# Gated delta rule: the key projection and its read-out moved ahead of the second masked decay

## The reference, cut to what matters

```
q, k, v = conv_silu(x @ w_q), conv_silu(x @ w_k), conv_silu(x @ w_v)   # causal convolution, 4 taps
q, k = l2norm(q), l2norm(k);  g, beta = gates from x @ w_a, x @ w_b
for t:  S = S * exp(g_t)
        delta = (v_t - k_t S) * beta_t
        S = S + k_t delta^T
        o_t = (q_t * scale) S
out = (rmsnorm(o) * silu(x @ w_g)) @ w_out
```

## Time and profile before

| | us |
|---|---|
| median of 3 runs | 4943.62 |
| lowest to highest | 4943.38 to 4948.53 |
| profiled execution | 4947.78 |
| its span, first to last instruction | 4945.9 |
| of it the quads, roughly | 42 to 1312 |

### The profile page before, as it was taken

How to read it: one execution, slowest core, us unless ns; L and a number is a source line. 1 busy time by engine, 2 the same in 40 slices (tenths; PEclk the granted TensorE clock), 3 DMA queues, 4 the chain that set the end, 5 groups by cost and what they waited for, 6 DMA issues and landing times. The chain is left out here.

```text
span 4945.9 us, 76468 instructions
## 1 busy us (share of the span) xinstructions
PE 3930.8 (79%) x20245; PEld 2366.6 (48%) x20365; DVE 3734.1 (75%) x6293; ACT 2549.7 (52%) x5336; POOL 2926.6 (59%) x2821
## 2 busy tenths in 40 slices
PE   5888888888578577576979964788888868888884
PEld 3666666666456356365447742333333323333332
DVE  5777777777377378366048857899999889999995
ACT  3555555555344244323246654566666456666662
POOL 2555555555454144143013344899999579999991
PEclk8999999989778878788999987999999989999997
DMA  1000000000000000000000000000000000000000
GB/s 50 9 9 8 9 9 9 8 9 8 16 0 0 21 0 0 12 0 24 0 18 1 1 14 10 0 0 0 0 0 0 8 0 0 0 0 0 0 0 14
DMA packets 90089, 33.37 MB, mean 7 GB/s; under 512 B 78032, under 2 KB 86113, under 8 KB 88929
## 3 DMA queue, kind: packets, MB, share of 16 engines
q1 hardware_dynamic: 89824, 30.17, 2.5%
HBM read 24.89 MB, written 5.24 MB: 6 GB/s over the span
## 5 line engine op out<-in xcount | busy, mean ns | idle before, releaser
L3284 POOL TENSOR_TENSOR dBx<-dtx,b_row 128x1024 f32<-128x1024 f32 x512 | 1219.4, 2382 | 3.9 <-ACT b_row L3250 3.9
L3318 DVE TENSOR_TENSOR_SCAN h<-banks,dBx 128x1024 f32<-128x1024 f32 x512 | 1168.5, 2283 | 19.2 <-ACT banks L3244 19.2
L3202 PE MATMUL banks<-hc,ident 128*128 128x512 f32 x2048 | 964.4, 593 | 0.0
L3244 ACT ACTIVATE banks<-dt,A 128x510 f32<-128x510 f32 x1024 | 661.7, 682 | 4.2 <-DVE h L3318 3.5
L3250 ACT ACTIVATE b_row<-banks 128x512 f32<-128x512 f32 x512 | 305.9, 597 | 574.8 <-PE banks L3186 574.8
L3202 PEld LDWEIGHTS banks<-hc,ident 128*128 128x128 f32 x2048 | 388.5, 190 | 272.3 <-issue 246.8
L3326 DVE TENSOR_TENSOR hc<-h,banks 128x768 f32<-128x768 f32 x512 | 478.6, 935 | 10.8 <-ACT c_row L3255 6.6
L3186 PE MATMUL banks<-bc_lo,selectors 128*128 128x512 bf16 x1024 | 391.3, 382 | 73.8 <-POOL b_row L3273 64.7
L3293 POOL TENSOR_TENSOR hc<-h,c_row 128x256 f32<-128x256 f32 x512 | 376.7, 736 | 55.9 <-ACT c_row L3255 28.7
L3185 PE MATMUL banks<-bc_hm_c,selectors 128*128 128x512 bf16 x506 | 195.1, 385 | 186.0 <-DVE hc L3326 185.6
L3185 PEld LDWEIGHTS banks<-bc_hm_c,selectors 128*128 (+1 forms) x512 | 49.2, 96 | 434.8 <-issue 434.5
(11 more groups left out here) (447 smaller groups left out, 9238.7 us busy)
## 6 DMA issues: line engine op xcount, KB each, us to landing
delta_blocks<-A_turned SPq DMA_DIRECT2D x256, 8.0 KB, 1.5
inv_turned<-delta_blocks SPq DMA_DIRECT2D x256, 8.0 KB, 1.8
blocks<-delta_blocks SPq DMA_DIRECT2D x32, 64.0 KB, 2.1
delta_blocks<-blocks_inv SPq DMA_DIRECT2D x32, 64.0 KB, 1.9
wh<-in_l1f_wh SPq DMA_DIRECT2D x1, 2048.0 KB, 9.0
wqkv<-in_l0f_wqkv SPq DMA_DIRECT2D x2, 768.0 KB, 4.1
residual<-in_x SPq DMA_DIRECT2D x1, 1024.0 KB, 4.7
wv<-in_l0a_wv SPq DMA_DIRECT2D x1, 1024.0 KB, 7.3
```

Of the source, the lines that this page charges most:

```text
L3202: i = nc.tensor.matmul(k.bank[e], k.ident[:], hc[:, s, e, :], start=False, stop=False)
L3244: i = nc.scalar.activation(a3[:, :, 1:], d3[:, :, 1:], ACT.Exp, scale=mem["A"][:, e, bass.ds(n, 1)])
L3284: nc.gpsimd.tensor_tensor(dBx[:, s % NS], dtx[:, :, bass.ds(c * SCH, SCH)], across(bsb[:, s % NS, :], SE), ALU.mult).then_inc(q["dbx_ready ...
L3318: v.tensor_tensor_scan(flat(h[:, s % NS]), flat(k.banks[:, at:at + SE, :]), flat(dBx[:, s]), 0.0, ALU.mult, ALU.add).then_inc(q["scanned"], 1)
```

## The change

On TensorE, `project(x0, 1)` (k) moves from behind `merge_y(x2, 1, ...)` to right behind `project(x0, 0)` (q), ahead of `decays(x0, 1)` and of `merge_y(x2, 1, ...)`. `turn_out`, which shares bank 5 with it, moves from behind `decays(x0, 1)` to ahead of `project(x0, 0)`. On ScalarE, `tap3(x0, 1)` moves ahead of `exp_decay(x0, 1)`. VectorE's, GpSimd's and SP's orders are as before, and no instruction is added or removed.

```diff
@@ tensor engine, step @@
+                    if x3 and x3[2] == 0 and not first(x3):
+                        turn_out(x1, x3[1] - 1)
                     if x0:
                         project(x0, 0)
+                        project(x0, 1)
                         decays(x0, 1)
-                    if x3 and x3[2] == 0 and not first(x3):
-                        turn_out(x1, x3[1] - 1)
                     if x2:
                         merge_y(x2, 1, 0)
                         merge_y(x2, 1, 1)
-                    if x0:
-                        project(x0, 1)
                     if x3:
                         turn_y(x0, x3, 1)
@@ scalar engine, step @@
                     if x0:
                         tap3(x0, 0)
                         exp_decay(x0, 0)
+                        tap3(x0, 1)
                         exp_decay(x0, 1)
-                        tap3(x0, 1)
```

## The result

| | before | after |
|---|---|---|
| median (14 runs each), us | 4942.59 | 4962.78 |
| lowest to highest | 4923.24 to 4954.62 | 4951.91 to 4978.26 |
| profiled execution | 4947.78 | 4958.38 |
| its span | 4945.9 | 4956.5 |

The ratio is 1.0047, 95% interval 1.0034 to 1.0061: about 20 us slower, where 3 us faster had been forecast. In the code of after, every line behind the change has a number lower by one (2535 for 2536, 2487 for 2488).

The account below looks back on a forecast made before the run. DVE's own list up to conv 1 was taken as the bound. Half-clock conv 1 waits -1.0, turn_out at half clock -3.0 and at full clock +1.0 summed to -3.0 us: 4940.6 us from 4943.6, range 4931 to 4950.

Parts of the forecast that it names:

- What bounds the block, and the hand order: Ordinary full-clock step: DVE runs without a gap through conv 1; k's read-out ends 0.78 us before conv 1 starts.
- the 0.63 worked out: PE, ordinary step: line 2027 starts 0.63 us later with k ahead, under 0.9 us of cover behind conv 0.
- The read-out: ACT: k's read-out between the exps adds no table load; second exp 0.85 us later, holding nothing up; value 0.
- PE is then done 0.4 us sooner than before with the same work, and waits for conv 0 anyway. Value: 0: PE behind line 2027, ordinary step: finishing 0.4 us earlier gains nothing; bounds nothing to 0.63 lost for 30 steps.
- the granted clock: PE's clock level: falls after waits at the end of the step before, untouched by the change; priced at 0.
- turn_out at half clock: Three half-clock steps with turned output: copy stops waiting, conv 0 1.4 us earlier, 1.0 kept each; -3.0 us, bounds -4.2 and 0.
- turn_out at full clock: Other four turned-output steps: k's projection waits for the copy, step_5 slips 0.25 us each; +1.0 us, bounds 0 and +4.0.
- (b): PE between q projection and line 2027: line 2027 becomes late and holds step_5; +16 us, 4957; chance 0.06.
- (c): PE's denser order holds the clock up, faster: -22 us if all half-clock stretches went, 4922; chance 0.11.

Follow-up runs that it names:

- e1: Before with only TensorE's part of the change, ScalarE's order as before: 4967.46 us, ratio to before 1.0052.
- e6: After, with the first of the third projection's two matmuls run twice, redundant work behind the joined wait: 4961.14 us, ratio to before 1.0041.
- e7: After, with the k projection behind the second decay and turned output but ahead of line 2027: 4959.23 us, ratio to before 1.0033.
- e2: Before with only ScalarE's part of the change, k's read-out ahead of the second exp: 4939.98 us, ratio to before 0.9995.
- e5: After, with the second masked decay computed twice only in steps without the turned output: 4946.89 us, ratio to before 1.0008.
- e8: Before, with the first masked decay of each step computed twice: 4944.53 us, ratio to before 1.0002.
- e10: Before, with the turned output ahead of the q projection and the first masked decay computed twice: 4947.27 us, ratio to before 0.9999.
- e12: Before, with the first of the k projection's two matmuls run twice: 4939.85 us, ratio to before 0.9992.
- e4: After, with the second masked decay computed twice in all steps to fill the joined wait: 4954.92 us, ratio to before 1.0024.
- e9: After, with only the second decay's first matmul run twice, in steps without the turned output: 4940.64 us, ratio to before 0.9993.
- e11: Before, with the second of the k projection's two matmuls left out: 4990.92 us, ratio to before 1.0097.
- e3: Before, with only the turned output moved ahead of the q projection: 4940.83 us, ratio to before 0.9998.

## Why the prediction was wrong

*What bounds the block, and the hand order.* Right. DVE's list up to conv 1 was the path, and the k projection was not late in ordinary steps. Line 2027 has no wait of its own and costs nothing; against conv 0 it is 0.29 us later (690.37 - 689.96 against 641.24 - 641.12), half of the 0.63 worked out, since matmuls in a row overlap more than I had counted. The read-out came out as said.

*"PE is then done 0.4 us sooner than before with the same work, and waits for conv 0 anyway. Value: 0"*, and *the granted clock*, "I therefore price it at 0": here it failed. The 0.49 us of waiting that was taken from ahead of line 2027 did not vanish but moved behind it, into one wait of 1.28 us. My own sum had it (line 2027 over at 642.99, line 2120 held by conv 0 until 643.94, so 0.95 us in one piece), and I put it at nothing. I looked only at where the clock had fallen in before, late in the step, and took it that the change touches no wait that matters to it. The runs show the opposite: all four kernels with this joined wait (after, e1, e6, e7) have 13 to 16 falls and are 0.33 to 0.52% slower; the eight others with the full result (e2 to e5, e8 to e10, e12) have 0 to 3 falls and, but for e4, ratios of 0.9992 to 1.0008. Filling the wait (e5, e9) undoes the loss, work beside it (e6) does not, and lengthening the wait by leaving work out of an otherwise unchanged order (e11) brings it about. The profiles are one execution each, but the clock of the whole execution is known for every run: averaged over its runs it is 0.902 to 0.907 in the four slow kernels and 0.896 in e11, and 0.913 to 0.916 in before and the eight others. In e4 it is 0.914, so its loss is not the clock's.

Two things stay open. Every kernel that joined the two waits also made their sum longer, 1.28 us against 1.01, and e11, which joined nothing, lengthened the sum to 1.44; so the runs do not tell one long wait from more waiting in all. And neither length alone foretells a fall: in five steps of after with the turned output, at full clock, k's projection waited 1.8 us in one piece for the copy, and no fall came in the middle of those steps; there the wait stands ahead of k and not of line 2120.

*The price of a fall.* In the traces, a step with a fall in its middle is 0.4 to 0.8 us longer if the fall is short (36.8 and 37.2 us from conv 1's end to the next, against 36.3) and some 2 us if it goes on, as in the step shown (701.16 - 694.01 against 650.62 - 645.16: 1.7). In this pair the waits for line 2030 are 10 us longer in all. The block's ends tell the same for all: 1285.5 to 1300.8 in the four slow kernels, mean 1294.6, and 1269.3 to 1288.2 in before, e2, e3, e5, e8, e9, e10 and e12, mean 1277.8. That is 17 us, near the difference of the medians; before's profiled execution is a late one of its kind, so the pair alone shows half of it. What makes the rest, beyond the waits for line 2030, was not taken apart step by step. Part of it goes with falls later in the step: counted the same way (130 to 1250 us, further than 5 us from conv 1's end) they are 11 to 15 in the four slow kernels, 12 in before and 6 to 11 in the eight others, and an ordinary step of before with such a fall takes 37.9 to 39.8 us from conv 1's end to the next, not 36.3.

*turn_out at half clock, "1.4 won", 1.0 kept of each.* Wrong, though small. In after such a step reads:

```profile
457.03 1.92 PE L1946 MATMUL banks<-norm_featmajor,wq 128*128 x4
459.10 0.84 ACT L2225 ACTIVATE qk<-banks,taps 128x256 f32<-128x256 f32 x2 [5.27 <-PE banks L1946]
459.19 0.42 DVE L2611 COPY block_out<-banks 128x256 f32 x1
...
459.97 2.76 DVE L2487 SCALAR_TENSOR_TENSOR qk<-banks,taps,qk 128x255 f32<-128x255 f32 x6 [0.35 <-ACT qk L2225]
461.55 1.91 PE L1954 MATMUL banks<-g_masked,tri 128*128 128x512 f32 x2
...
464.85 0.28 DVE L2524 COPY steps<-banks 32x128 f32<-32x128 f32 x1 [2.12 <-PE banks L2027]
```

The copy no longer waits and conv 0 comes early, as said, but the clock stayed at half for k's projection and the decays too, and step_5 waited 2.12 us for line 2027. From the block transpose to `turn_64`, right behind conv 1, it is 468.89 - 457.37 = 11.5 us; in the step of the earlier trace rows it was 608.59 - 597.32 = 11.3.

*turn_out at full clock, "+0.25" each.* Not there: k's projection did wait for the copy, but from transpose to conv 1's end it is 9.2 us in both, so the bound of 0 was the right end.

*The rivals.* The result lies in the part, over 4953.5, that had a chance of 0.07, given nearly all to (b). (b) had the sign, and its mechanism did appear in two steps of after (4.2 us) and in e4; it is not what made the loss, for e7 has no such wait and is as slow. (c) named the right resource with the wrong sign: I argued from the wait that is closed and not from the one that opens. The Trainium skill (TensorE: Matmul & The Clock Gate, section HAM oscillation) warns of TensorE waiting between pieces of work; its example is of waits for DMA of 3 to 5 us. The runs agree with its direction, and here much shorter waits go with the falls: 1.28 us in one piece in after, 0.49 and 0.95 us in e11.

## What to carry to other kernels

Moving work ahead of a wait on an engine that is not the bound does not remove the wait; ask where it comes out again and how long the joined one is. For TensorE list the waits by place, and if a reordering joins or lengthens them just ahead of work that others wait for, do not put the granted clock at nothing: give a rival in which that work runs at half clock a chance and a price. A cheap test is to fill the wait with idempotent work: if time comes back with more work, it was the clock; if it comes back only in part, as in e4, look for the added work on the path.

## What the runs showed of the hardware

- Leaving out one 128 x 256 product in each step made the kernel 50 us slower (4990.92 against 4940.90), and running it twice cost nothing (4939.85 against 4942.79). Between the two, the granted clock over 130 to 1250 us went from 0.89 to 0.98.
- In the step shown the fall comes behind the wait, not in it: the wait ends at 692.78, the clock falls at about 693.3, and over the 6.7 us at 0.50 TensorE was busy for all 6.7.
- The mean granted clock is a poor measure of time by itself: e8 and e10 had 0.98 against before's 0.95 in the profiled stretch, and 0.916 against 0.915 and 0.913 over all runs, and gained nothing.
